# A four-layer graph network on one core: step table by products, norms folded into weights, work moved into the gather loops

## The chip, the core and the metric

The kernel runs on one core of a Trainium2 chip, as one program. The time is the device time of that core in microseconds. Before the change the runs took 7613.0, 7617.18 and 7625.78 us, median 7617.18.

## The reference

6250 nodes with 128 features and 106,250 edges, sorted by destination, pass through four layers, each added to its input and normalised: `x = layernorm(x + layer(x))`. The change concerns the first layer (two SAGE convolutions with batch norm) and what is prepared for it:

```
def _sage_conv(h, src, dst, n_nodes, Wl, bl, Wr):
    msg = jnp.take(h, src, axis=0)
    agg = jax.ops.segment_sum(msg, dst, num_segments=n_nodes)
    cnt = jax.ops.segment_sum(jnp.ones_like(src, dtype=h.dtype), dst, num_segments=n_nodes)
    agg = agg / jnp.clip(cnt, 1.0)[:, None]
    return agg @ Wl + bl + h @ Wr
def _batchnorm(h, gamma, beta):
    mu = jnp.mean(h, axis=0)
    var = jnp.mean((h - mu) ** 2, axis=0)
    return (h - mu) * jax.lax.rsqrt(var + EPS) * gamma + beta
...
h = _sage_conv(x, src, dst, n, Wl0, bl0, Wr0)      # 128 -> 256
h = _batchnorm(jax.nn.relu(h), g0, b0)
h = _sage_conv(h, src, dst, n, Wl1, bl1, Wr1)      # 256 -> 256
h = _batchnorm(jax.nn.relu(h), g1, b1)
return jax.nn.relu(h @ Wp + bp)                    # 256 -> 128
```

The other three (a Moebius aggregation, an equivariant convolution with weights from 64 edge features, graph attention) follow on the same edges and are untouched, except that edge weights for the last two are computed inside the SAGE loops.

## The kernel before

Nodes lie in 49 tiles of 128 (`TILES`, `NP` = 6272 columns), edges in 831 tiles of 128. A *step* is one pair of a node tile and an edge tile that meet; there are 880 (`STEPS`), in bodies of 8 (110 `BODIES`). The stages run one after the other, with a barrier between: `setup`, `sage_layer` for layers 0 and 1, `moebius`, `equivariant`, `gat`.

`setup` builds the pointer of each node into the edges: 49 VectorE passes compare the first destination of every edge tile (`firsts`, 832 columns) with the nodes of a tile, 49 GpSimd gathers fetch the edge tile in question (L336), and 49 more passes count in it. The pointers go through DRAM and back; from them come the degrees, the boundaries of node tiles, the step table (`stT`, node tile of a step; `stE`, edge tile), then gathers of `src` and `dst` for each step and transposes give `srcS` and `dstS`. A counting sort of the nodes by degree (`oh`, `cum`, `rank`) gives the place of each. Beside it x is split in three bf16 parts (L403 and on), each pass over all 6272 columns, and stored as `x_split`.

`sage_layer` has for each step an indirect DMA that GpSimd issues (L700): 128 rows of the split table, 16 slots deep (`SLOTS`). At every fourth step GpSimd waits until TensorE's `step_done` has freed slots. TensorE multiplies the three parts with a 128x128 one-hot matrix (L789: 3 matmuls in layer 0, 6 in layer 1). VectorE makes the one-hots for four steps at a time (L200) and adds each product into `agg` (L884). Between steps TensorE computes the edge weights for later layers (L798, L808, in layer 0 also L802), ScalarE moves them (L731). TensorE's, ScalarE's and VectorE's bodies are hardware loops (`fours`); GpSimd's 880 gathers are written out.

A tail follows. VectorE multiplies `agg` by 1/degree (L921). For 14 chunks (`NCH`) of 448 columns (`CH`) and two halves TensorE forms `agg` Wl + own Wr (L829, L831), ScalarE adds the bias and applies relu (L757), VectorE takes statistics (L937), then normalises both halves (L950). Layer 0 then transposes each tile (L841) and splits it in three parts (VectorE L957, L959; ScalarE L768, L770), stores `y_split`; meanwhile GpSimd scatters the sorted node table (L704). Layer 1 at its start loads that table (`sback`, copied at L867) and clears `span_src`; in its tail GpSimd reduces the largest degree (L709), VectorE plans the spans of `moebius`, GpSimd gathers 49 `span_src` (L1009), TensorE projects tile by tile (two products with Wp and one with the bias, L844, L845), VectorE applies relu and adds x (L962), and `LayerNorm` ends the stage. The order of work on each engine is the order of the code; engines meet at semaphores.

## Time and profile before

| | |
|---|---|
| median of three runs | 7617.18 us |
| the profiled execution | 7613.2 us |
| its span, first to last instruction | 7611.2 us |
| VectorE busy | 4112.7 us (54%) |
| GpSimd busy | 5148.9 us (68%) |
| TensorE busy | 2675.4 us (35%) |
| ScalarE busy | 1491.7 us (20%) |

In the rows below PE is TensorE, PEld its weight load, DVE VectorE, ACT ScalarE, POOL GpSimd and SP the engine that issues the remaining DMAs. L200 is line 200 of the kernel before; `out<-in` are the buffers by the program's names. A windows row gives a stretch in us from the span's start, its length, then for each engine its busy us and, in brackets, its instructions, then TensorE's granted clock as a share of full speed, the mean busy share of 16 DMA engines, and GB/s. A timeline row gives start, duration, engine, line, operation, names, the count, and in brackets how long the engine stood idle before it and what ended that. Issuing a DMA counts as "issue". A row of one line's instructions gives count, shortest/median/longest ns, first and last start. What is averaged over the span says little here: the stages have different limits, so the rows are taken stage by stage.

### The profile page before, as it was taken

How to read it: one execution, taken by the hardware profiler on the slowest of the kernel's cores; microseconds unless marked ns; L12 is line 12 of the kernel's file. 1: busy time of each engine (PE TensorE's matmuls, PEld its weight loads, DVE VectorE, ACT ScalarE, POOL GpSimd, SP SyncE). 2: the span in 40 equal slices, each digit the busy share in tenths (PEclk: the TensorE clock that was granted, in tenths of full speed). 3: DMA queues.
4: the chain of work that ended last, by engine and by line, in shares of the span. 5: the costliest groups of instructions: out<-in, count | busy, mean ns of one | idle time of the engine just before them, and what ended most of it. 6: DMA issues, size and time to landing. Idle time of an engine off the chain costs nothing. (4 is left out here: it accounts for less than half of the span.)

```text
span 7611.2 us, 86798 instructions
## 1 busy us (share of the span) xinstructions
PE 2675.4 (35%) x13121; PEld 1768.7 (23%) x13121; DVE 4112.7 (54%) x10643; ACT 1491.7 (20%) x5205; POOL 5148.9 (68%) x5017
## 2 busy tenths in 40 slices
PE   0466666756677673000000005666667100000000
PEld 0244444435455442000000003333335100000000
DVE  5344443454444433676677866777777414444465
ACT  0000000120000010121222104777774000000000
POOL 3277777757777742777777564777774477777765
PEclk9666555667777775555555557788878555555555
DMA  2544444356666621222222113333332322222211
GB/s 36 101 126 123 126 123 125 88 171 198 197 198 198 195 62 45 49 46 48 48 47 48 35 26 95 101 101 101 101 101 56 84 55 52 52 52 52 53 39 32
DMA packets 433517, 681.95 MB, mean 90 GB/s; under 512 B 159150, under 2 KB 266608, under 8 KB 433120
## 3 DMA queue, kind: packets, MB, share of 16 engines
q0 software_dynamic: 203280, 470.84, 24.5%
q10 hardware_dynamic: 127152, 159.46, 6.3%
q1 hardware_dynamic: 102944, 50.32, 2.9%
q14 instruction: 120, 0.98, 0.0%
q8 instruction: 21, 0.34, 0.0%
HBM read 584.78 MB, written 95.44 MB: 89 GB/s over the span
## 5 line engine op out<-in xcount | busy, mean ns | idle before, releaser
L1116 POOL DMA_INDIRECT mb_rows<-x_tab,mb_idx x906 | 1009.1, 1114 | 342.5 <-issue 276.4
L789 PE MATMUL ps<-onehot,rows 128*128 128x128 bf16 x7920 | 945.4, 272 | 732.7 <-DMA rows<-x_split,srcS 329.5
L884 DVE TENSOR_TENSOR agg<-agg,ps 128x128 f32 (+1 forms) x1760 | 623.7, 354 | 954.6 <-PE ps L789 806.3
L1414 POOL DMA_INDIRECT eq_frow<-f_tab,srcS x880 | 894.6, 1017 | 356.8 <-issue 267.9
L1732 POOL DMA_INDIRECT gt_rows<-h_tab,gt_idx x906 | 931.8, 1028 | 298.7 <-issue 273.9
L700 POOL DMA_INDIRECT rows<-x_split,srcS x880 | 864.8, 983 | 379.3 <-issue 244.9
L700 POOL DMA_INDIRECT rows<-y_split,srcS x880 | 840.6, 955 | 333.2 <-issue 245.8
L1436 ACT ACTIVATE eq_pb<-eq_wrow 128x64 f32<-128x64 f32 (+1 forms) x3520 | 864.1, 334 | 430.9 <-DVE eq_msg L1553 366.7
L1476 PE MATMUL eq_ps<-eq_msg,eq_onehot 128*128 128x320 f32 x1760 | 739.6, 581 | 435.2 <-DVE eq_onehot L200 423.8
L789 PEld LDWEIGHTS ps<-onehot,rows 128*128 128x128 bf16 x7920 | 631.6, 120 | 1106.2 <-DVE agg L884 738.9
L1464 PE MATMUL eq_ps<-ident,eq_x 128*128 128x128 f32 x49 | 14.0, 291 | 1686.9 <-DMA eq_m<-in_L_gnn_W_l_D 1686.9
L1476 PEld LDWEIGHTS eq_ps<-eq_msg,eq_onehot 128*128 128x128 f32 x1760 | 425.9, 254 | 748.4 <-DVE eq_acc L1561 570.7
L200 DVE TENSOR_TENSOR onehot<-iota,dstS 128x512 bf16<-128x512 f32 x440 | 305.3, 694 | 275.3 <-issue 263.0
L1561 DVE TENSOR_TENSOR eq_acc<-eq_acc,eq_ps 128x320 f32 x880 | 425.0, 483 | 51.6 <-issue 29.8
L808 PE MATMUL ps<-w2d,hT 128*128 128x256 f32 x880 | 415.8, 624 | 0.0
L1464 PEld LDWEIGHTS eq_ps<-ident,eq_x 128*128 128x128 f32 x49 | 7.3, 151 | 1688.7 <-issue 1687.2
L731 ACT ACTIVATE wrow<-ps 128x512 f32<-128x512 f32 x220 | 131.3, 597 | 1268.7 <-PE ps L808 1268.7
L1845 DVE TENSOR_TENSOR gt_alpha<-gt_rows,gt_scores_in 128x196 f32<-128x196 f32 (+5 forms) x36 | 9.5, 264 | 671.5 <-DMA gt_rows<-h_tab,gt_idx 671.0
L1179 DVE TENSOR_TENSOR mb_prod<-mb_rows,mb_xd 128x256 f32<-128x256 f32 (+4 forms) x128 | 140.5, 1098 | 401.8 <-DMA mb_rows<-x_tab,mb_idx 322.3
L1153 ACT ACTIVATE mb_rows<-mb_rows,mb_gm 128x128 f32<-128x128 f32 x906 | 268.5, 386 | 361.6 <-DVE mb_gm L1222 361.6
L1009 POOL DMA_INDIRECT span_src<-in_src,span_at x147 | 161.0, 1095 | 243.3 <-DVEq L1805 158.5
L1548 DVE TENSOR_TENSOR eq_msg<-eq_pb,eq_frow 128x512 f32<-128x512 f32 x220 | 152.4, 693 | 259.5 <-DMA eq_frow<-f_tab,srcS 248.2
(395 smaller groups left out, 5021.9 us busy)
## 6 DMA issues: line engine op xcount, KB each, us to landing
eq_wrow<-w_tab ACTq DMA_DIRECT2D x223, 264.0 KB, 3.0
w_tab<-wrow ACTq DMA_DIRECT2D x220, 264.0 KB, 2.7
es<-in_side ACTq DMA_DIRECT2D x220, 136.0 KB, 2.6
mb_rows<-x_tab,mb_idx POOLq DMA_INDIRECT x906, 2.6
gt_rows<-h_tab,gt_idx POOLq DMA_INDIRECT x906, 2.5
rows<-x_split,srcS POOLq DMA_INDIRECT x880, 2.7
rows<-y_split,srcS POOLq DMA_INDIRECT x880, 3.1
eq_frow<-f_tab,srcS POOLq DMA_INDIRECT x880, 2.6
```

What stands on the lines that cost most here:

```text
L200: return dve.tensor_tensor(onehot[:, 4 * half:4 * half + 4], broadcast(s["iota"][:], four, 1), broadcast(s["dstS"][:, bass.ds(4 * b, 4)], ...
L700: pool.indirect_dma_start(rows[:, n % SLOTS, :], None, table, bass.IndirectOffsetOnAxis(ap=s["srcS"][:, n:n + 1], axis=0)).then_inc(gather ...
L789: last = pe.matmul(ps[:, u % 4, f * P:(f + 1) * P], rows[:, slot, at:at + P], onehot[:, u], start=(part == 0), stop=(part == 2))
L808: last = pe.matmul(ps[:, 7, 2 * n * P:(2 * n + 2) * P], hT[:, n * P:(n + 1) * P], w2d[:], start=True, stop=True)
L884: dve.tensor_tensor(into, into, ps[:, u % 4, 0:W].rearrange("p (k n) -> p k n", n=P), ALU.add).then_inc(added, 1)
L1116: pool.indirect_dma_start(rows[:, r, n, :], None, t["x1"], bass.IndirectOffsetOnAxis(ap=idx[:, r, n:n + 1], axis=0)).then_inc(gathered[r][ ...
L1153: act.activation(rows[:, r, n, 0:D], rows[:, r, n, 0:D], ACT.Copy, scale=gm[:, n:n + 1]).then_inc(scaled_ready, 1 if n + 1 < UPTO[p] else ...
L1414: pool.indirect_dma_start(frow[:, n % SLOTS, :], None, t["f"], bass.IndirectOffsetOnAxis(ap=s["srcS"][:, n:n + 1], axis=0)).then_inc(gathe ...
L1436: last = act.activation(pb[:, r % 2, u, f].rearrange("p c w -> p (c w)"), wrow[:, r, bass.ds(at, 1), lo:lo + 64].rearrange("p o f -> p (o ...
L1476: pe.matmul(ps[:, 4 * r + u, 0:MC], onehot[:, 4 * r + u], msg[:, r, u], start=True, stop=True).then_inc(step_done, 1)
L1561: dve.tensor_tensor(into, into, ps[:, 4 * (r % 2) + u, 0:MC], ALU.add).then_inc(added, 1)
L1732: pool.indirect_dma_start(rows[:, r, n, :], None, t["h"], bass.IndirectOffsetOnAxis(ap=idx[:, r, n:n + 1], axis=0)).then_inc(gathered[r][g ...
```

## The change

**Setup.** The inputs get an array `first`, the first destination of each edge tile, copied to all partitions. One counting pass over 896 columns gives for each of 49 tiles how many edge tiles start below it; from it comes `reach`, a 0/1 matrix of tile by step, whose column sum (a product with ones) less 1 is `stT`; `stE` is the step's number less `stT`. `srcS` and `dstS` are products of the edge arrays with one-hot matrices (`pick`) of `stE`, in four quarters. The split of x is cut in 7 groups and shared by ScalarE and VectorE. Pointers, degrees and the sort leave setup.

**First layer** (`sage_first`). One more matmul with one column for each step counts edges, in column P of `agg`. In bodies 4 to 52 TensorE also forms x Wr + bias of a tile (`h0`). The tail goes by tile: product with `wl`, VectorE multiplies by 1/degree and adds `h0`, ScalarE and VectorE split relu of it; `y_split` holds the unnormalised values, and `h0` is stored too.

**Second layer** (`sage_second`). In the loop `h0` is loaded and transposed (bodies 2 to 26), its statistics taken, and the norm folded into `wl`, `wr`, `cvec` and `bwl`; the own part (three 448-column products for each of 28 half chunks) follows at even bodies from 34. Histogram and placement of the sort are spread over bodies 2 to 14 and from 35 on. The scatters of the sorted table, its reload, the span plan stand behind this layer's loop. The dense tail takes the mean in 14 pieces, two products for each half chunk, and folds the second norm into `wps` and a bias that VectorE adds. Loops of TensorE and ScalarE (both layers) and of VectorE (second layer) are written out. The core of the diff (the old code stands above):

```diff
-            "ptr": dram("ptr_tab", (NP + P,), I32),
             "rc": dram("rc_tab", (NP,)),
-            "stepT": dram("step_node_tile", (EROWS,), I32),
-            "stepE": dram("step_edge_tile", (EROWS,), I32),
+            "h0": dram("h0_tab", (NP, HID)),
...
+            pe.wait_ge(reach_ready, 1)
+            for h in range(2):
+                last = pe.matmul(ps[:, h, 0:2 * QUART], s["ones_h"][0:TILES, :], reach[0:TILES, h * 2 * QUART:(h + 1) * 2 * QUART],
+                                 start=True, stop=True)
+            last.then_inc(counted, 1)
+            for q in range(4):
+                pe.wait_ge(pick_ready, q + 1)
+                for n in range(2):
+                    for j, c in enumerate(chunks[q]):
+                        last = pe.matmul(ps[:, 2 + q, 256 * n:256 * n + QUART], edge_f[:, n, c], pick[q][:, j], start=(j == 0),
+                                         stop=(j == len(chunks[q]) - 1))
+                last.then_inc(picked, 1)
...
+            dve.wait_ge(first_in, 16)
+            do(dve.tensor_scalar(junk[0:TILES], first_i[0:TILES], part128[0:TILES], 0.0, ALU.is_lt, ALU.add,
+                                 accum_out=cnt[0:TILES]))
+            do(dve.tensor_scalar(bound[0:TILES], cnt[0:TILES], -1.0, 0.0, ALU.add, ALU.max))
+            do(dve.tensor_tensor(bound[0:TILES], bound[0:TILES], part_f[0:TILES], ALU.add))
+            do(dve.tensor_scalar(reach[0:TILES], col_f[0:TILES], bound[0:TILES], None, ALU.is_ge))
+            dve.sem_inc(reach_ready, 1)
+            dve.wait_ge(edges_in, 32)
+            for n in range(2):
+                do.put(dve.tensor_copy(edge_f[:, n], edge_i[:, n]))
+            dve.wait_ge(counted, 1)
+            for h in range(2):
+                do.put(dve.tensor_scalar(stT[:, h * 2 * QUART:(h + 1) * 2 * QUART], ps[:, h, 0:2 * QUART], -1.0, None, ALU.add))
+            do.sync()
+            do(dve.tensor_tensor(stE[:], col_f[:], stT[:], ALU.subtract))
+            for q in range(4):
+                for j, c in enumerate(chunks[q]):
+                    do.put(dve.tensor_scalar(pick[q][:, j], stE[:, q * QUART:(q + 1) * QUART], row_f[:, c:c + 1], None, ALU.is_equal))
+                do.sync()
+                dve.sem_inc(pick_ready, 1)
...
+            for g in range(GROUPS + 1):
+                if g < GROUPS:
+                    dve.wait_ge(hi_ready, g + 1)
+                    dve.tensor_tensor(rest[:, seven(g)], xin[:, seven(g)], xs[:, seven(g), 0], ALU.subtract).then_inc(rest_ready, 1)
+                if g < 4:
+                    steps(g)
+                if g:
+                    dve.wait_ge(mid_ready, g)
+                    dve.tensor_tensor(xs[:, seven(g - 1), 2], rest[:, seven(g - 1)], xs[:, seven(g - 1), 1],
+                                      ALU.subtract).then_inc(xs_ready, 1)
...
+                    pe.matmul(ps[:, u % 4, P:P + 1], onehot[:, u], s["ones_h"][:, 0:1], start=True, stop=True)
+                    for part in range(3):
+                        last = pe.matmul(ps[:, u % 4, 0:P], rows[:, slot, part * D:(part + 1) * D], onehot[:, u],
+                                         start=(part == 0), stop=(part == 2))
                     last.then_inc(step_done, 1)
...
                 last.then_inc(w_psum, 1)
...
+                if PRE <= k < PRE + TILES:
+                    if k == PRE:
+                        pe.wait_ge(setup_in, N_SETUP)
+                    n = k - PRE
+                    pe.matmul(ps[:, 5, HID:2 * HID], xT[:, n * P:(n + 1) * P], wr[:], start=True, stop=False)
+                    pe.matmul(ps[:, 5, HID:2 * HID], s["ones"][0:1, :], bl[:], start=False, stop=True).then_inc(pre_psum, 1)
+                steps(k, 4, 6)
...
+            pe.wait_ge(added, STEPS + 4)
             for n in range(TILES):
...
+                if n >= 4:
+                    pe.wait_ge(summed, n - 3)
+                pe.matmul(ps[:, n % 4, 0:HID], agg[:, n, 0:P], wl[:], start=True, stop=True).then_inc(dense_ready, 1)
...
+            dve.wait_ge(pre_ready, TILES)
+            for n in range(TILES + 2):
+                if n < TILES:
+                    dve.wait_ge(dense_ready, n + 1)
+                    dve.scalar_tensor_tensor(h0[:, n], ps[:, n % 4, 0:HID], rc[:, n:n + 1], h0[:, n], ALU.mult,
+                                             ALU.add).then_inc(summed, 1)
+                if 1 <= n <= TILES:
+                    dve.wait_ge(hi_ready, n)
+                    if n > 3:
+                        dve.wait_ge(staged, n - 3)
+                    dve.scalar_tensor_tensor(yrest[:, (n - 1) % 3], h0[:, n - 1], 0.0, ystage[:, (n - 1) % G, 0], ALU.max,
+                                             ALU.subtract).then_inc(rest_ready, 1)
+                if n >= 2:
+                    dve.wait_ge(mid_ready, n - 1)
+                    dve.tensor_tensor(ystage[:, (n - 2) % G, 2], yrest[:, (n - 2) % 3], ystage[:, (n - 2) % G, 1],
+                                      ALU.subtract).then_inc(staged, 1)
...
+        TURN = 2
+        HIST = TURN + QUADS4 + 2
+        CONST = TURN + PAIRS + 4
+        OWN = CONST + 3
+        PLACE = OWN + 1
+        PLACED = PLACE + 2 * QUADS4 + 1
...
+            pool.wait_ge(rank_ready, 1)
+            for n in range(TILES):
+                pool.indirect_dma_start(t["srt"][:, :], bass.IndirectOffsetOnAxis(ap=s["rank"][:, n:n + 1], axis=0),
+                                        s["sval"][:, n, :], None).then_inc(sorted_out, 16)
+            pool.wait_ge(deg_ready, 1)
+            pool.partition_all_reduce(dmax[:], s["sdeg"][:], P, bass.bass_isa.ReduceOp.max).then_inc(dmax_ready, 1)
+            pool.wait_ge(plan_ready, 1)
+            for n in range(TILES):
+                span_sources(pool, a, s, n).then_inc(span_in, 16)
...
+            def turn_pair(j):
+                pe.wait_ge(yT_ready, j)
+                for m in range(2):
+                    n = 2 * j + m
+                    if n < TILES:
+                        pe.wait_ge(hin_in[n % 4], 16 * (n // 4) + 16)
+                        for f in range(2):
+                            last = pe.transpose(ps[:, 6, 256 * f + P * m:256 * f + P * m + P], hin[:, n % 4, half(f)], s["ident"][:])
+                last.then_inc(turned, 1)
+
+            def own_part(j):
+                c, f = j // 2, j % 2
+                pe.wait_ge(pre_ready, j)
+                if f == 0:
+                    pe.wait_ge(sign_ready, c + 1)
+                for k in range(2):
+                    pe.matmul(ps[:, 6, 0:CH], wr[:, k, half(f)], yT[:, k, chunk(c)], start=(k == 0), stop=False)
+                pe.matmul(ps[:, 6, 0:CH], bwl[:, half(f)], sign[:, c % 2], start=False, stop=True).then_inc(pre_psum, 1)
...
+                if k >= OWN and (k - OWN) % 2 == 0 and (k - OWN) // 2 < 2 * NCH:
+                    if k == OWN:
+                        pe.wait_ge(w_scaled, 1)
+                    own_part((k - OWN) // 2)
+                if k >= PLACE and (k - PLACE) % 2 == 0 and (k - PLACE) // 2 < QUADS4:
+                    b = (k - PLACE) // 2
+                    pe.wait_ge(place_in, b + 1)
+                    many = min(4, TILES - 4 * b)
+                    for m in range(many):
+                        place = ps[:, 4, m * P:(m + 1) * P]
+                        pe.matmul(place, s["ones_h"][:], cum[:, m], start=True, stop=False)
+                        last = pe.matmul(place, s["tri"][:], oh[:, m], start=False, stop=True)
+                    last.then_inc(place_ready, 1)
+                steps(k, 4, 8)
...
+            pe.wait_ge(pre_ready, 2 * NCH + 1)
+            for n in range(2 * NCH):
+                c, f = n // 2, n % 2
+                if f == 0:
+                    pe.wait_ge(mean_ready, c + 1)
+                if n >= 4:
+                    pe.wait_ge(sum_ready, n - 3)
+                for k in range(2):
+                    last = pe.matmul(ps[:, n % 4, 0:CH], wl[:, k, half(f)], agg[:, k, chunk(c)], start=(k == 0), stop=(k == 1))
...
+                if 0 <= k - TURN < QUADS4:
+                    for m in range(key_hot(k - TURN)):
+                        do(dve.tensor_tensor(cum[:, 0], cum[:, 0], oh[:, m], ALU.add))
...
+            for k in range(BODIES):
+                h, i = k % BUFS, k // BUFS
                 for u in range(U):
+                    b = 2 * k + u // 4
                     if u % 4 == 0:
...
+                        tiles = node_tiles(dve, s, b)
+                        if 2 <= b + 1 < 2 * BODIES:
+                            one_hots(b + 1)
+                    add(U * k + u, tiles[u % 4])
                     if u == 1:
...
                         dve.wait_ge(es_in[h], 16 * i + 16)
...
+                        if i:
                             dve.wait_ge(w_out[h], 16 * i)
...
+                        dve.tensor_copy(wrow[:, h, :, D:WW],
+                                        es[:, h, 2 * P:SIDE].rearrange("p (n f) -> p n f", n=WB)).then_inc(e4_ready, 1)
+                    if u == 3:
+                        side(k)
...
+            mean(0)
+            mean(1)
+            dve.wait_ge(pre_ready, 2 * NCH + 1)
             for c in range(NCH):
+                if c + 2 < NCH:
+                    mean(c + 2)
                 for f in range(2):
-                    dve.wait_ge(dense_free, 2 * c + f + 1)
-                    do.put(dve.bn_stats(stats[:, f, c], h_[:, f, c * CH:min((c + 1) * CH, N)]))
+                    n = 2 * c + f
+                    dve.wait_ge(dense_ready, n + 1)
+                    dve.tensor_tensor(yT[:, f, chunk(c)], ps[:, n % 4, 0:CH], yT[:, f, chunk(c)], ALU.add).then_inc(sum_ready, 1)
+                    if c:
+                        tally(n - 2)
...
+            def order():
+                dve.wait_ge(sorted_in, 16)
+                do.put(dve.tensor_copy(s["perm"][:], sback[:, :, 0]))
+                do.put(dve.tensor_copy(s["eptr"][:], sback[:, :, 1]))
+                do(dve.tensor_copy(s["sdeg"][:], sback[:, :, 2]))
+                dve.sem_inc(deg_ready, 1)
...
+            order()
             for n in range(TILES):
...
+                dve.wait_ge(projected, n + 1)
+                dve.wait_ge(x_in[n % G], 16 * (n // G + 1))
+                do(dve.tensor_tensor(v[:, n], ps[:, n % G, 0:D], bias, ALU.add))
+                dve.scalar_tensor_tensor(v[:, n], v[:, n], 0.0, xin[:, n % G], ALU.max, ALU.add).then_inc(staged, 1)
+                if n == G:
+                    plan()
```

GpSimd, from the first layer's gathers to the end of the second layer; before:

```order
L693 UNCONDITIONAL_BRANCH
L700 DMA rows<-x_split,srcS 128x384 x880
L704 DMA sorted_nodes<-sval,rank_i 6272x4 x49
L540 UNCONDITIONAL_BRANCH
L76 ISA
L693 UNCONDITIONAL_BRANCH
L700 DMA rows<-y_split,srcS 128x768 x880
L709 ISA
L709 ISA dmax<-sdeg 128x49
L1009 DMA span_src<-in_src,span_at 128x48 x49
```

and after the change (names of the layers' buffers now begin with `s_`):

```order
L521 UNCONDITIONAL_BRANCH
L526 DMA s_rows<-x_split,srcS 128x384 x880
L433 UNCONDITIONAL_BRANCH
L76 ISA
L838 UNCONDITIONAL_BRANCH
L843 DMA s_rows<-y_split,srcS 128x768 x880
L847 DMA sorted_nodes<-sval,rank_i 6272x4 x49
L850 ISA
L850 ISA s_dmax<-sdeg 128x49
L1241 DMA span_src<-in_src,span_at 128x48 x49
```

The 49 scatters moved from behind the first layer's gathers to behind the second's, ahead of the reduction (`dmax`) and the span gathers.

VectorE, around a one-hot in the second layer's body; before:

```order
L884 TENSOR_TENSOR agg<-agg,ps 128x2x128
L193 TENSOR_LOAD stepT
L193 ISA x2
L200 TENSOR_TENSOR onehot<-iota,dstS 128x512
L884 REGISTER_ALU
L884 ISA
L884 TENSOR_TENSOR agg<-agg,ps 128x2x128
```

and after, in one of bodies 2 to 14:

```order
L1023 TENSOR_TENSOR s_agg<-s_agg,s_ps 128x2x128
L1028 TENSOR_TENSOR s_oh<-iota,s_key 128x512
L1049 TENSOR_TENSOR s_cum<-s_cum,s_oh 128x128 x4
L194 TENSOR_LOAD stepT
L194 ISA x2
L201 TENSOR_TENSOR s_onehot<-iota,dstS 128x512
L1023 REGISTER_ALU
L1023 ISA
L1023 TENSOR_TENSOR s_agg<-s_agg,s_ps 128x2x128
```

A one-hot of sort keys and four additions now stand between the fourth addition of a body and the next one-hot.

TensorE, a body of the second layer; before:

```order
L798 MATMUL ps<-es,w1d 128x256
L784 ISA
L785 ISA
L789 MATMUL ps<-onehot,rows 128x128 x6
L785 REGISTER_ALU
L789 MATMUL ps<-onehot,rows 128x128 x6
L785 REGISTER_ALU
L789 MATMUL ps<-onehot,rows 128x128 x6
L785 REGISTER_ALU
L789 MATMUL ps<-onehot,rows 128x128 x6
L805 REGISTER_ALU
L808 MATMUL ps<-w2d,hT 128x256 x2
```

and after, in a body that also holds an own part:

```order
L943 MATMUL s_ps<-s_es,s_w1d 128x256
L916 MATMUL s_ps<-s_onehot,s_rows 128x128 x24
L948 MATMUL s_ps<-s_w2d,s_hT 128x256 x2
L936 MATMUL s_ps<-s_yT,s_wr 128x448 x2
L937 MATMUL s_ps<-span_src,s_bwl 128x448
L916 MATMUL s_ps<-s_onehot,s_rows 128x128 x24
```

The own part's three products stand behind the side products, between a body's first four steps and its last four (24 matmuls each); register work of the loop is gone.

## Rows read from the trace of the kernel before

**Rows 1.** Windows by stage: length, busy PE, PEld, DVE, ACT, POOL; clock, DMA, GB/s

```profile
0.00:326.70 326.70, 56.49 (x218) 34.94 (x218) 147.70 (x331) 0.68 (x2) 74.63 (x75) 0.88 0.30 39
326.70:1463.20 1136.50, 733.44 (x3734) 499.47 (x3734) 461.45 (x1432) 108.44 (x221) 864.81 (x880) 0.59 0.45 130
1463.20:1594.90 131.70, 75.89 (x216) 37.09 (x216) 71.98 (x142) 53.13 (x129) 58.62 (x49) 0.68 0.23 79
1594.90:2710.50 1115.60, 755.99 (x5922) 559.23 (x5922) 542.46 (x1214) 108.42 (x221) 840.66 (x881) 0.77 0.67 197
2710.50:2981.50 271.00, 180.18 (x536) 114.36 (x536) 103.94 (x384) 19.16 (x37) 46.70 (x51) 0.67 0.11 30
2981.50:7611.20 4629.70, 873.46 (x2495) 523.59 (x2495) 2785.19 (x7142) 1201.83 (x4597) 3263.45 (x3084) 0.59 0.25 61
```

**Rows 2.** GpSimd's timeline at the borders of the stages

```profile
326.70 0.94 POOL L700 DMA_INDIRECT rows<-x_split,srcS  x1 [107.90 <-POOLq L77]
...
350.28 0.94 POOL L700 DMA_INDIRECT rows<-x_split,srcS  x1 [3.92 <-PE ps L789]
...
1594.91 0.98 POOL L700 DMA_INDIRECT rows<-y_split,srcS  x1 [58.45 <-POOLq L77]
...
1621.94 0.94 POOL L700 DMA_INDIRECT rows<-y_split,srcS  x1 [7.28 <-PE ps L789]
...
2710.45 0.47 POOL L709 PARTITION_ALL_REDUCE dmax<-sdeg  x1 [0.21 <-issue]
...
2981.49 0.94 POOL L1104 DMA_INDIRECT mb_xd<-x_tab,perm  x1 [186.74 <-PEq L1043]
```

**Rows 3.** The gathers of the first loop, by source line

```profile
L700 POOL DMA_INDIRECT rows<-x_split,srcS x880: 940/946/1462, 326.7 to 1462.0; - x176
```

**Rows 4.** Timelines of VectorE and GpSimd, setup and second loop

```profile
80.64 6.69 DVE L404 TENSOR_TENSOR rest<-xin,xs 128x6272 f32<-128x6272 f32 x1
80.75 7.41 POOL L336 DMA_INDIRECT drow<-in_dst,blk_i  x1 [0.30 <-issue]
...
2002.56 0.69 DVE L200 TENSOR_TENSOR onehot<-iota,dstS 128x512 bf16<-128x512 f32 x1 [0.51 <-issue]
2002.62 1.44 POOL L700 DMA_INDIRECT rows<-y_split,srcS  x1 [0.30 <-issue]
```

**Rows 5.** VectorE's timeline at the start of setup

```profile
9.29 0.17 DVE L374 MEMSET ones<- 128x128 f32 x1 [9.15 <-POOL last_i L331]
...
18.34 1.08 DVE L396 TENSOR_SCALAR_CACHE_REDUCE junk<-firsts,node_f 128x832 f32<-128x832 f32 x1 [3.33 <-POOL firsts L333]
```

**Rows 6.** Windows in the second tail: dense products, then the projection

```profile
2728.00:2817.00 89.00, 86.84 (x224) 43.55 (x224) 20.66 (x61) 16.73 (x29) 46.27 (x49) 0.97 0.09 14
2828.00:2919.00 91.00, 90.37 (x290) 68.54 (x289) 14.45 (x50) 0.00 (x0) 0.00 (x0) 0.50 0.11 31
```

**Rows 7.** DMA issues of the page: count, us from issue to landing

```profile
rows<-x_split,srcS POOLq DMA_INDIRECT x880, 2.7
```

**Rows 8.** VectorE's timeline in the first tail

```profile
1467.25 6.69 DVE L921 TENSOR_TENSOR agg<-agg,rcb 128x6272 f32<-128x6272 f32 x1
...
1530.92 0.43 DVE L959 TENSOR_TENSOR ystage<-yrest,ystage 128x256 bf16<-128x256 f32 x1 [0.47 <-ACT ystage L770]
1531.26 0.42 DVE L957 TENSOR_TENSOR yrest<-ps,ystage 128x256 f32<-128x256 f32 x1
...
1590.28 0.42 DVE L959 TENSOR_TENSOR ystage<-yrest,ystage 128x256 bf16<-128x256 f32 x1 [0.47 <-ACT ystage L770]
```

**Rows 9.** VectorE's timeline: second tail, and the table's load

```profile
2714.94 13.29 DVE L921 TENSOR_TENSOR agg<-agg,rcb 128x6272 f32<-128x6272 f32 x2
...
2918.41 0.29 DVE L962 SCALAR_TENSOR_TENSOR yT<-ps,xin 128x128 f32<-128x128 f32 x1 [1.58 <-PE ps L845]
...
1601.09 0.20 DVE L867 COPY perm<-sback 128x49 int32<-128x49 int32 x1 [6.33 <-DMA sback<-sorted_nodes]
```

**Rows 10.** The scatters of the sorted table, by source line

```profile
L704 POOL DMA_INDIRECT sorted_nodes<-sval,rank_i x49: 965/969/6632, 1463.2 to 1535.5; - x49
```

1153 lines of the change are left out of this document (600 added, 553 removed).

## The prediction, made before the changed kernel was run

> **What bounds the kernel now.** I first cut the span at the stages' borders with the windows view [rows 1], taking the borders from GpSimd's timeline [rows 2]. The reader is to see six stretches: setup up to the first gather (326.7 us), the first layer's loop (1136.5), its tail (131.7), the second layer's loop (1115.6), its tail (271.0), and the rest (4629.7), which the change doesn't touch. The change can only win or lose in the first five, 2981.5 us together.
>
> In both loops the bound is GpSimd. Each of 880 gathers has a median of 946 ns [rows 3] and is followed by 0.30 us of issue, the gap that the timeline shows before most of them [rows 2]. That makes 1.249 us, and 880 of them 1099 us. The loops take 1136.5 and 1115.6, so 37.5 and 16.6 us lie above that floor. Of these 3.6 and 7.0 us are one wait each near the start, where the 17th gather waited for TensorE's first steps (3.92 and 7.28 us less the usual 0.30) [rows 2]. The rest, 34 and 10 us, are gathers that took longer. [Rows 4] show why: a VectorE tensor_tensor of 6.69 us that reads two SBUF operands began at 80.64, and the indirect DMA begun at 80.75 lasted 7.41 us, to the end of that pass. In the loop the 0.69 us one-hot of 2002.56 stretched the gather of 2002.62 to 1.44 us. The additions into `agg`, which read PSUM and SBUF, leave no such trace. TensorE is busy 733 of 1136 and 756 of 1116 us, VectorE 461 and 542 [rows 1], and their order only matters where it makes GpSimd wait.
>
> In setup and in the tails GpSimd is not the bound: a chain of VectorE, TensorE and round trips through DRAM is.
>
> **Setup.** All of the old chain goes: 49 counting passes of 1.08 us over 832 columns [rows 5] plus 49 over the fetched blocks, 49 gathers of blocks, the pointer table's way to DRAM and back, the step table's, and the node sort. The new chain: VectorE starts as before at 9.3 us, when GpSimd's iotas are there [rows 5]. One counting pass over 896 columns costs 1.2 us by the same row. I estimate about 2 us for bounds and `reach`, 1.3 for two casts, 1.5 for `stT`, 1 for `stE`, 3.5 for 11 compares of 224 columns, and 4 for the small tables: 24 us. Then x is split in 7 groups. A pass over 6272 columns takes 6.69 us [rows 4], so 0.96 per group, two of them on VectorE and two now on ScalarE beside it; four groups also carry two copies of 224 columns (0.7 us). That is 4 x 2.6 + 3 x 1.9 + 1 = 17 us, to 41. The products on TensorE (22 of 224 columns, about 0.4 us each at the high clock, 0.8 at the low, half of the 448-column ones in [rows 6]) need 9 to 17 us from about 18 on and lie beside it. The last group's store, the barrier and the first issue take some 8 us: first gather at 50, against 326.7. Bounds: 40 if the small operations are cheaper, 72 if ScalarE or TensorE gates the groups. **-277**, between -255 and -287.
>
> **The two start waits.** In the new first layer the one-hots precede the wait for the attention weights, and the loads of side data are issued first; 16 gathers take 20 us and TensorE's first steps should be done by then. In the second layer the wait for the sorted table and the clearing of `span_src` are gone from VectorE's head, leaving its 10.5 us clearing of `agg`. Both waits vanish, **-10**; if they stay, 0.
>
> **What moves into the loops.** First layer: one matmul with one column for each step, and 49 bodies with two 256-column products. Second layer: 98 transposes, 28 own parts of three 448-column products, 98 small placement products, and on VectorE two sets of 13 key one-hots and 98 cumulative additions. TensorE: the old second tail ran 224 instructions in 86.84 us [rows 6], two for each 448-column product, so 0.78 each: 84 x 0.78 = 65 us, with the small ones about 120 us at the high clock, 240 at the low; idle are 360 us [rows 1]. First layer: about 90 for the products and 90 for the counts, idle 403. Both fit on the average. The largest lump, side product and own part at the low clock, is 2 + 4.7 us; GpSimd gathers up to 12 steps (15 us) ahead of TensorE, less 3 for the landing (2.7 [rows 7]), so the lump is covered. The order rows show these lumps stand between step 3 and step 4 of a body. ScalarE is busy 108 us of either loop and can take copies.
>
> What isn't covered is the shared port. Now 220 one-hots per loop cost 34 us in the first (0.155 each) and 10 in the second (0.045): the phase against the gather decides. The count matmul makes a step's result some 0.1 us later, towards the gather's start, where a one-hot hurts more; lumps of TensorE scatter the phase. I take +8 in the first loop. The second gets 26 key one-hots, 98 short additions and 13 masks with two SBUF operands, plus a less lucky phase: +14. Together **+22**. Bounds: -43 if no one-hot ever meets a gather; +155 if each of 440 costs 0.45 us as the one in [rows 4] did.
>
> The Trainium skill speaks against moving such work here: "SBUF — State Buffer", section "SBUF: two separate sides", says that a VectorE operation with two SBUF inputs and a GpSimd operation take their shared port pair exclusively, each for its whole length, and the loser stands still. The trace agrees [rows 4]. By the rule alone all added two-operand time (18 + 26 + 9 us) could come on top, some +53; what it costs here hangs on whether the gather begins inside it.
>
> **First tail.** Before: mean, 56 products, statistics, normalisation, transposes, split. The statistics, normalisation and transposes go. For each tile VectorE now has three passes of 256 columns. Such passes started 0.34 us apart where none waited (1530.92 to 1531.26 [rows 8]), but the pair took 1.24 us with ScalarE's hop; the new loop is skewed over three tiles so that the hop lies beside other work: 3 x 0.35 = 1.05 us, 49 + 2 rounds 54 us. The stores grow from 192 to 320 KB a tile, 16.1 MB in all. The second loop moves 197 GB/s at a DMA share of 0.67 [rows 1], so 294 at full share and 55 us. Both limits meet; I take 56. Before it stand 4.1 us of last steps (1463.2 to 1467.25 [rows 8]) and an estimated 2.1 of small passes for the reciprocals, behind it 7.5 for a last store of 7 tiles and the barrier (4.2 before, from 1590.7 to 1594.9 [rows 2, 8]). 69.7 instead of 131.7: **-62**. With stores at 197 GB/s it would be 82 + 14, so -36; without any waiting -66.
>
> **Second tail.** Here two things move against each other. VectorE and TensorE: the mean pass (13.3 us [rows 9]) is cut into 14 pieces beside TensorE, half of the dense products are gone (1.55 us a half chunk instead of 3.1), normalisation (7 us) and the bias product too. VectorE then bounds with 0.96 for the mean and 0.56 for each of two additions and two statistics of 448 columns (13.29 us for 2 x 6272 columns make 1.06 ns each, and an estimated 0.08 to start), 3.2 us a chunk: 4.5 + 2 + 45 + 9 for the rest up to the projection = about 60 us after the last gather. But the 49 scatters of the sorted table, in the old first tail hidden beside dense work, now stand behind the last gather on GpSimd's queue [rows 2], and VectorE's wait for the table stands ahead of every projection tile. They took 58.6 us of work [rows 1] and 49 x 0.30 of issue, 73.3 together, of which 11 were two of them held beside long passes (median 0.969, the longest 6.632 [rows 10], beside the 6.69 us pass of 1467.25 [rows 8]); at the median it is 62, and I take 67. Landing 2.5, loading the table back 6.8 (VectorE waited 6.33 of it [rows 9]), unpacking 0.7: 77. So the table, not the products, releases the projection, 17 us late. The projection ran 49 tiles in 91 us with 6 instructions each at the 1.2 GHz level (clock 0.50) [rows 6]; now 4: 1.24 us a tile. Seven tiles are ready, 42 x 1.24 + 1 = 53: 130. VectorE's plan of 5 us lies inside TensorE's seven-tile lead, and the 49 `span_src` gathers (61 us) end at about 149. From the last tile to the next stage 62.8 us are as before (2918.7 to 2981.5 [rows 2, 9]): 193 instead of 271, **-78**. If the clock were high there, VectorE's 0.65 us a tile would bound and it would be -103; if the scatters took 78, -65.
>
> **Sum.** -277 - 10 + 22 - 62 - 78 = -405 us. The profiled execution took 7613.2 us (span 7611.2), so 7208; the median of the runs is 7617.2, 4 us above, so I predict 7210.
>
> **Rivals.** (a) The shared port bites: the new step time puts the one-hots just ahead of each gather, 0.45 instead of 0.1 us, in both loops. For it: the one-hot of [rows 4] and the port rule; against: each delay moves the gather itself, and neither loop of before sat there. 7208 + 133 = about 7340. (b) TensorE's lumps are not covered: if each of the 28 own parts and 49 pre-products costs its low-clock length in full (28 x 4.7 + 49 x 1.9), that is +220, half of it likely: 7320. Against: the 12-step lead. (c) Everything lucky: no contention, high clock in the projection: 7210 - 65 - 25 = 7120. (d) Slower than before. TensorE's, ScalarE's and the second layer's VectorE bodies, looped before, are now written out 110 times. If each body cost a stall of fetching code on TensorE beyond its idle time, so that a body of 8 steps takes more than 10.1 + 1.9 us, the 220 bodies would eat all 405. At 12.5 us it is +528: 7740. Against it: GpSimd's 880 gathers were written out too, and their gap stays at 0.30 [rows 2]; TensorE has 3 us idle per body.
> The Trainium skill, "Runtime: NRT & Kernel Launch", section "Instruction fetch mechanics", says that fetching is sequential and prefetched and that taken branches break it, so by it the written-out code costs nothing, against (d). The even gaps of the gathers agree; no row shows TensorE that way.
>
> **Chances.** Forecast 0.74 (7150 to 7270), (a) 0.09, (b) 0.08, (c) 0.06, (d) 0.03. The range for 8 in 10 reaches towards (a), (b) and (c): 7140 to 7310. Faster by over 0.2% (15 us, about what a measurement of this kernel can tell from none): 0.96; within 0.01; slower 0.03.
>
> **What would show it.** First gather at about 50 us; the 17th gather of each loop without a wait; loops of 1141 and 1123 us with GpSimd's gap at 0.30 and the excess in gather durations beside one-hots and key one-hots; the second loop's first gather 70 us after the first's end; in the second tail 49 scatters with VectorE waiting for `sback` until some 76 us, then a tile each 1.24 us at clock 0.50; everything behind that as before within 5 us. I am wrong if GpSimd waits for TensorE in the loops by more than a few us, if setup ends after 75 us, or if the second tail is above 215.

## The result, and the profile after

The changed kernel took 7212.69 us (median of four, 7207.55 to 7217.6) against 7616.94 for the kernel before on the same chip: ratio 0.9468, 95% interval 0.9451 to 0.9484. The forecast was 7210. The profiled execution took 7207.55 us, its span is 7205.6, and its windows, cut at the same borders as [rows 1], read (length, busy PE, PEld, DVE, ACT, POOL, clock, DMA share, GB/s):

```profile
0.00:49.60 49.60, 11.59 (x46) 10.05 (x46) 30.13 (x66) 14.62 (x17) 1.56 (x9) 0.85 0.65 190
49.60:1181.20 1131.60, 774.83 (x4807) 546.10 (x4807) 458.18 (x1430) 126.46 (x270) 863.28 (x880) 0.65 0.46 128
1181.20:1260.30 79.10, 36.85 (x110) 17.82 (x108) 55.25 (x159) 35.98 (x99) 0.00 (x0) 0.80 0.89 212
1260.30:2403.50 1143.20, 787.28 (x6307) 583.13 (x6308) 623.49 (x1474) 145.06 (x290) 875.10 (x881) 0.80 0.67 201
2403.50:2574.80 171.30, 77.87 (x332) 53.52 (x328) 126.44 (x479) 21.72 (x38) 100.84 (x99) 0.71 0.22 48
2574.80:7205.60 4630.80, 874.25 (x2495) 526.73 (x2495) 2780.40 (x7142) 1201.83 (x4597) 3258.69 (x3084) 0.59 0.25 61
```

| stage | before | forecast | measured | off by |
|---|---|---|---|---|
| setup | 326.7 | 50 | 49.6 | -0.4 |
| first loop | 1136.5 | 1141 | 1131.6 | -9 |
| first tail | 131.7 | 69.7 | 79.1 | +9 |
| second loop | 1115.6 | 1123 | 1143.2 | +20 |
| second tail | 271.0 | 193 | 171.3 | -22 |
| rest | 4629.7 | 4629.7 | 4630.8 | +1 |

So the total is right to 3 us, while four of the five changed stages are off by 9 to 22 us and cancel. These four are what the experiments are about.

GpSimd's timeline shows the first surprise, one row in each loop. Both waits of the 17th gather, 3.92 and 7.28 us in [rows 2], are gone; instead the first gather of each loop lasts 8.04 and 14.32 us, where it took 0.94 and 0.98:

```profile
49.62 8.04 POOL L526 DMA_INDIRECT s_rows<-x_split,srcS  x1 [37.25 <-POOLq L77]
...
1260.31 14.32 POOL L843 DMA_INDIRECT s_rows<-y_split,srcS  x1 [79.51 <-POOLq L77]
```

VectorE at the same time, with two one-hots directly behind the clearing of `agg`:

```profile
1262.77 10.51 DVE L1009 MEMSET s_agg<- 128x12544 f32 x1 [2.56 <-issue]
1273.19 1.22 DVE L201 TENSOR_TENSOR s_onehot<-iota,dstS 128x512 bf16<-128x512 f32 x2
```

In the kernel before the same clearing stood from 1607.5 to 1618.0, gathers were issued beside it, and none took more than 0.95 us; there a semaphore wait stood between it and the one-hots. The row's start has to be read with care: VectorE cleared 256 columns just before in 0.27 us, and at that rate 12544 take about 13.1 us (an estimate), which is the 10.51 us of the row and the 2.56 us in front of it. So the clearing began, by that estimate, at about 1260.2, just ahead of the gather.

The second is in the first tail. The rounds of three VectorE passes follow at 1.06 us each, as forecast, up to the eighth tile, and there VectorE stands still; the second row is from the view of ScalarE's waits in that stretch (us in total, times, longest):

```profile
1208.69 0.42 DVE L703 SCALAR_TENSOR_TENSOR s_yrest<-s_h,s_ystage 128x256 f32<-128x256 f32 x1 [13.94 <-ACT s_ystage L564]
```

```profile
ACT s_ystage L564 <- DMA y_split<-s_ystage: 15.6, 2, 14.8
```

ScalarE waits for the first tile's store. From 1186 to 1208 us the DMA view has this line,

```profile
DMA packets 7011, 1.00 MB, mean 46 GB/s; under 512 B 6379, under 2 KB 7010, under 8 KB 7010
```

and of SyncE's issues in it these two:

```profile
y_split<-s_ystage SPq DMA_DIRECT2D x6, 192.0 KB, 10.8
rc_tab<-s_rc SPq DMA_DIRECT2D x1, 24.5 KB, 21.6
```

`rc_tab` are the reciprocal degrees, 24.5 KB in elements of 4 bytes: 6272 of the packets. SyncE now stores them ahead of the first tile, and they took 21.6 us to land.

The third is the projection. VectorE gets the table 75 us behind the last gather, as forecast (76), after 13.75 us of waiting; but then the tiles do not take 1.24 us each:

```profile
2478.32 0.20 DVE L1176 COPY perm<-s_sback 128x49 int32<-128x49 int32 x1 [13.75 <-DMA s_sback<-sorted_nodes]
```

The windows over the projection, same columns as above:

```profile
2488.60:2494.00 5.40, 4.79 (x22) 4.79 (x23) 4.92 (x20) 0.00 (x0) 4.11 (x5) 0.50 0.40 100
2494.00:2500.00 6.00, 6.00 (x50) 6.00 (x49) 5.62 (x24) 0.00 (x0) 4.62 (x5) 0.89 0.55 134
2500.00:2507.00 7.00, 7.00 (x63) 6.99 (x63) 6.55 (x28) 0.00 (x0) 5.33 (x6) 1.00 0.61 152
```

After the pause the clock is at the 1.2 GHz level (0.50) and rises to 2.4 GHz within the projection; in [rows 6] it stood at 0.50 for all of 91 us. At the high level a tile takes 0.53 us, and VectorE's two passes are what sets it.

For the loops I compared each gather with its median of 946 ns and added up what lies above it, the held first gathers apart. It is 24.4 us in the first loop (before 32.9) and 30.0 in the second (before 9.0). Sorted by the VectorE operation that ran when the gather began, 25 of the second loop's 30 us stand beside one-hots: 84 gathers that a one-hot lengthened by more than 0.05 us, 25.2 us in all, 0.30 each. With 1099 us of floor and the 7.1 and 13.4 us of the held gathers that makes 1130.5 and 1142.4, within 1 us or so of the loops (1131.6 and 1143.2).

### The profile page after: what moved, and what is told of

Same layout as the page of the kernel before. It is cut to its first block and busy times, and to the rows that moved or that the text cites. A ratio compares the mean times of both kernels' runs of the same rounds, so it can differ in the third digit from the quotient of the medians.

```text
span 7205.6 us, 84694 instructions
## 1 busy us (share of the span) xinstructions
PE 2562.7 (36%) x14090; PEld 1737.3 (24%) x14090; DVE 4073.9 (57%) x10750; ACT 1545.7 (21%) x5308; POOL 5099.5 (71%) x4952
## 5 line engine op out<-in xcount | busy, mean ns | idle before, releaser
L843 POOL DMA_INDIRECT s_rows<-y_split,srcS x880 | 875.1, 994 | 347.3 <-issue 251.0
L526 POOL DMA_INDIRECT s_rows<-x_split,srcS x880 | 863.3, 981 | 305.2 <-issue 251.4
L1023 DVE TENSOR_TENSOR s_agg<-s_agg,s_ps 128x256 f32 x880 | 369.7, 420 | 446.9 <-PE s_ps L916 314.8
L916 PE MATMUL s_ps<-s_onehot,s_rows 128*128 128x128 bf16 x5280 | 488.7, 251 | 324.7 <-DMA s_rows<-y_split,srcS 302.1
L659 DVE TENSOR_TENSOR s_agg<-s_agg,s_ps 128x129 f32 x880 | 254.6, 289 | 524.4 <-PE s_ps L585 432.6
L916 PEld LDWEIGHTS s_ps<-s_onehot,s_rows 128*128 128x128 bf16 x5280 | 385.0, 114 | 467.4 <-DMA s_rows<-y_split,srcS 408.0
L201 DVE TENSOR_TENSOR s_onehot<-iota,dstS 128x512 bf16<-128x512 f32 x440 | 304.7, 693 | 217.7 <-issue 171.2
L585 PE MATMUL s_ps<-s_onehot,s_rows 128*128 128x128 bf16 x2640 | 359.5, 272 | 0.0
```

Of the source, the lines that this page charges most:

```text
L201: return dve.tensor_tensor(onehot[:, 4 * half:4 * half + 4], broadcast(s["iota"][:], four, 1), broadcast(s["dstS"][:, bass.ds(4 * b, 4)], ...
L526: pool.indirect_dma_start(rows[:, n % SLOTS, :], None, t["xs"], bass.IndirectOffsetOnAxis(ap=s["srcS"][:, n:n + 1], axis=0)).then_inc(gath ...
L585: last = pe.matmul(ps[:, u % 4, 0:P], rows[:, slot, part * D:(part + 1) * D], onehot[:, u], start=(part == 0), stop=(part == 2))
L843: pool.indirect_dma_start(rows[:, n % SLOTS, :], None, t["ys"], bass.IndirectOffsetOnAxis(ap=s["srcS"][:, n:n + 1], axis=0)).then_inc(gath ...
L916: last = pe.matmul(ps[:, u % 4, half(f)], rows[:, slot, at:at + P], onehot[:, u], start=(part == 0), stop=(part == 2))
L1023: dve.tensor_tensor(into, into, ps[:, n % 4, 0:HID].rearrange("p (k n) -> p k n", n=P), ALU.add).then_inc(added, 1)
```

## The experiments

Where an experiment's effect is small, its stages are compared by the profile, from the start of one gather to another, since medians from different chips scatter by some 10 us. "Less than the changed kernel" below is the difference of its gain over the kernel before on its own chip to the 404 us of the changed kernel.

**A wait between the clearing and the one-hots** (`e1_wait_zero`).

```diff
             dve.sem_inc(added, 4)
+            dve.wait_ge(agg_zero, 1)
             def compare(b):
...
+            dve.wait_ge(agg_zero, 1)
             one_hots(0)
             one_hots(1)
-            dve.wait_ge(agg_zero, 1)
```

> The changed kernel with VectorE's wait for the end of the clearing of agg moved ahead of the first two one-hots, in both SAGE layers; nothing else. In the changed kernel the first gather of each loop took 8.04 and 14.32 us instead of 0.94. Theory Q (queued lock): a one-hot with two SBUF operands that stands ready right behind the clearing holds the port from then on, and the gather waits for both; then with the wait between them both first gathers take under 1.7 us, the loops are 1124 and 1130 us (now 1131.6 and 1143.2) and the time falls by about 20 us. Theory M (the clearing itself holds the gather): both stay at 8 and 14 us, no change. Theory F (the first gather behind a barrier is slow in itself in this code): no change either.

Measured: 7188.03 us, ratio 0.9444 (0.9427 to 0.9460), 17 us less than the changed kernel. GpSimd and VectorE at the second loop's start:

```profile
1255.40 0.95 POOL L843 DMA_INDIRECT s_rows<-y_split,srcS  x1 [79.65 <-POOLq L77]
```

```profile
1257.86 10.51 DVE L1009 MEMSET s_agg<- 128x12544 f32 x1 [2.56 <-issue]
1268.40 1.29 DVE L201 TENSOR_TENSOR s_onehot<-iota,dstS 128x512 bf16<-128x512 f32 x2
```

Clearing and one-hots are as long as ever; only the wait stands between, and the gather takes 0.95 us (1.30 in the first loop), as do the ones behind it that run beside the clearing. From first to last gather's start the loops went from 1130.2 to 1124.6 and from 1141.9 to 1130.2 us. Neither the clearing itself nor the first gather in itself is the cause: what makes the difference is whether an operation stands ready behind the clearing. How such an operation can hold a gather before it has started itself, the runs don't show. In the second loop the excess of the other gathers stayed, at 31.6 us.

**The reciprocal degrees as rows** (`e2_rc_rows`).

```diff
-            sp.dma_start(t["rc"].rearrange("(t p o) -> p t o", p=P, o=1), rc[:].unsqueeze(2),
-                         allow_slow_non_contiguous=True).then_inc(rc_out, 16)
...
+                if n == 6:
+                    sp.wait_ge(rc_ready, 2)
+                    sp.dma_start(t["rc"].rearrange("(t p) -> t p", p=P), rcT[0:TILES, :]).then_inc(rc_out, 16)
...
+                    pe.transpose(ps[0:TILES, 6, 2 * P:3 * P], rc[:], s["ident"][:]).then_inc(rc_turned, 1)
```

> The changed kernel with the reciprocal degrees transposed on TensorE and stored as 49 rows of 512 bytes behind the seventh tile's store, instead of 6272 elements of 4 bytes ahead of the first. The first tail is 79.1 us in the changed kernel, with one stall of 13.9 us at the eighth tile, where ScalarE waits for the first tile's store. Theory R: the stall is the small elements ahead of it in SyncE's queue; then it goes, the tail is 66 to 70 us, and the time falls by 9 to 13. Theory B (the bytes: 16.1 MB at the rate of the engines): the stall only spreads over the later tiles, the tail stays above 76 us and the time within 3 us.

Measured: 7190.07 us, ratio 0.9447 (0.9431 to 0.9463), 15 us less. The same wait of ScalarE, and the packets of the same 22 us:

```profile
ACT s_ystage L566 <- DMA y_split<-s_ystage: 1.4, 2, 0.8
```

```profile
DMA packets 4252, 5.12 MB, mean 233 GB/s; under 512 B 295, under 2 KB 4251, under 8 KB 4251
```

From the last gather of the first loop to the first of the second it is 66.9 us instead of 80.4. The 16 MB alone are hidden: theory R holds. The edit changes two things, though, the form of the store and its place behind the seventh tile, and no run takes them apart; that the form matters is read from the 21.6 us that these 24.5 KB took in the changed kernel.

**The table's wait moved into the projection** (`e3_table_late`).

```diff
+                if n == TABLE - 4:
+                    sp.wait_ge(sorted_out, 16 * TILES)
+                    sp.dma_start(sback[:], t["srt"].rearrange("(t p) f -> p t f", p=P)).then_inc(sorted_in, 16)
...
             for n in range(TILES):
+                if n == TABLE:
+                    order()
```

> The changed kernel with the wait for the sorted table (order) at projection tile 28 instead of ahead of the first, and SyncE's load of it moved to the same place in its row. In the changed kernel VectorE waits 13.75 us for the table while TensorE has 7 tiles ready. Theory T (the table is what releases the projection): the wait shrinks below 2 us, the last projection tile ends 10 to 13 us earlier, and since the span gathers (61 us from the plan on) keep their place and end ahead of the LayerNorm, the second tail falls from 171 to about 160. Rival C (clock): the pause is what left TensorE at its high level in the projection; without it the tiles take 1.24 us at the low level as before the change (49 tiles, 61 us), and the tail gets longer, about 185.

Measured: 7202.94 us, ratio 0.9463 (0.9447 to 0.9479): no difference that the runs can tell. By the profile the tail, from last gather to the next stage's first, fell from 172.6 to 167.1, where about 160 was expected. TensorE's timeline and a window:

```profile
2467.69 17.62 PE L1003 MATMUL s_ps<-s_wps,s_yT 128*128 128x128 f32 x124
2489.64 8.23 PE L1003 MATMUL s_ps<-s_wps,s_yT 128*128 128x128 f32 x48 [4.32 <-DVE s_agg L1196]
```

```profile
2465.00:2482.00 17.00, 15.86 (x107) 14.53 (x107) 13.15 (x44) 0.00 (x0) 11.53 (x12) 0.82 0.33 62
```

The 13.75 us wait is gone, but 4.3 us of it came back: VectorE waited 4.42 us for a load of x, and SyncE's loads stand behind its wait for the scatters. Half of the gain was there, not all. Rival C is out: without the pause the clock is 0.82.

**One-hots of the second loop as four tensor_scalar** (`e4_scalar_hots`).

```diff
+    for u in range(4):
+        last = dve.tensor_scalar(onehot[:, 4 * half + u], s["iota"][:], s["dstS"][:, 4 * b + u:4 * b + u + 1], None, ALU.is_equal)
+    last.then_inc(ready, 1)
...
-                one_hot(dve, s, onehot, b, b % 2).then_inc(onehot_ready, 1)
+                four_hots(dve, s, onehot, b, b % 2, onehot_ready)
```

> The changed kernel with each one-hot of the second SAGE layer (one tensor_tensor of 512 columns with two SBUF operands) made by four tensor_scalar of 128 columns, which read one tensor and a number for each partition. Port theory: only operations with two SBUF operands hold a gather; the one-hots account for some 25 of the 30.8 us by which the second loop's gathers exceed 946 ns, the key one-hots and placement for the other 5, and the first gather's 14.3 us go too, since no one-hot with two operands stands behind the clearing: second loop 1143 to about 1105, the time down by 35 to 40 us. Rival L (any long VectorE operation beside a gather's start holds it): the excess stays at 25 or grows with the longer passes (4 x 0.28 instead of 0.69), no gain or a few us slower.

Measured: 7175.38 us, ratio 0.9430 (0.9415 to 0.9446), 30 us less. The excess beside one-hots fell from 25.2 to 1.7 us (24 gathers by more than 0.05 us), that of the whole loop from 30.0 to 7.4. But the first gather was held as before, by operations with only one tensor operand:

```profile
L850 POOL DMA_INDIRECT s_rows<-y_split,srcS x880: 942/946/13858, 1262.8 to 2382.6; - x176
```

```profile
1275.65 1.53 DVE L201 TENSOR_SCALAR s_onehot<-iota,dstS 128x128 bf16<-128x128 f32 x8
```

So the port theory is right on the loop's excess and wrong on the first gather: one-hots with one tensor operand behind the clearing hold it too. It ended at 1276.63, before the last of the eight one-hots (1277.18), so not all of them were waited for. Whether the small excess is owed to the kind of the operations or to their length, the next one asks.

**The same with four short tensor_tensor** (`e10_short_pairs`).

```diff
-        last = dve.tensor_scalar(onehot[:, 4 * half + u], s["iota"][:], s["dstS"][:, 4 * b + u:4 * b + u + 1], None, ALU.is_equal)
+        last = dve.tensor_tensor(onehot[:, 4 * half + u], s["iota"][:], s["dstS"][:, 4 * b + u:4 * b + u + 1].broadcast_to([P, P]),
+                                 ALU.is_equal)
```

> The changed kernel with each one-hot of the second loop made by four tensor_tensor of 128 columns, both operands in SBUF, instead of one of 512; beside the kernel that made them by four tensor_scalar, where the gathers stretched beside a one-hot fell from 25 to 2 us. Theory K (the kind of the operation: only two tensors from SBUF hold a gather): the four stand one behind the other for 0.85 us, and the excess of the gathers beside them stays at 20 us or more; second loop 1140 to 1145. Theory L (the length: a gather is held to the end of the operation that runs, and gets in between two short ones): the excess falls to 6 us or less as with tensor_scalar, second loop about 1120 with the first gather's 14 us still in it.

This one and `e9_one_row` ran on a chip where the kernel before took 8740.59 us, and the engines have issue gaps that no other run shows; their times say little, 8347.31 us and a ratio of 0.9556 (0.9497 to 0.9615), and the loop's length can't be compared. The gathers' durations can: their median is 949 ns, and beside one-hots the excess is 4.5 us in 42 gathers, 0.11 each. In the first loop of the same run, where the one-hots still had 512 columns, 69 gathers lost 0.28 each, and in the changed kernel's second loop 84 lost 0.30. VectorE and GpSimd at one such meeting:

```profile
2005.65 0.90 DVE L201 TENSOR_TENSOR s_onehot<-iota,dstS 128x128 bf16<-128x128 f32 x4 [0.24 <-PE s_ps L924]
```

```profile
2005.72 1.05 POOL L851 DMA_INDIRECT s_rows<-y_split,srcS  x1 [0.31 <-issue]
```

0.90 us of two-operand work, and the gather that began 0.07 us into it lost 0.10. Theory L holds in the main: the length of one operation decides, not the sum of those that follow each other. The kind may have a smaller share. Over all gathers that began beside a one-hot, lengthened or not, the mean loss is 0.22 us with one of 512 columns (117 gathers), 0.05 with four tensor_tensor of 128 (111) and 0.02 with four tensor_scalar (149), the middle one from the other chip.

**Own parts three times over** (`e5_own_thrice`).

```diff
+                for again in range(3):
+                    for k in range(2):
+                        pe.matmul(ps[:, 6, 0:CH], wr[:, k, half(f)], yT[:, k, chunk(c)], start=(k == 0), stop=False)
+                    last = pe.matmul(ps[:, 6, 0:CH], bwl[:, half(f)], sign[:, c % 2], start=False, stop=True)
```

> The changed kernel with each own part in the second loop (three products of 448 columns) issued three times over, so a lump of 9 instead of 3 at 28 places, 168 more products of about 0.78 us at the high clock. Theory of the forecast (12 gathered steps cover a lump): a lump grows from 2.3 to 7 us at the high clock and 14 at the low; GpSimd's waits for TensorE grow by less than 10 us and the loop stays within 1143 to 1155. Rival (b) of the prediction (lumps are not covered, each costs its length): 28 x 4.7 = 130 us more in the second loop, about 1270.

Measured: 7235.86 us, ratio 0.9524 (0.9509 to 0.9538), 43 us more than the changed kernel. From first to last gather the second loop took 1174.3 us, 32 more. GpSimd's wait for TensorE in it (total, times, longest; 16.7 us in 55 times in the changed kernel, which is the usual 0.3 each):

```profile
POOL s_rows L843 <- PE s_ps L916: 61.1, 84, 3.2
```

The rival's 130 us are out, and so are my 10: the cover ends between a lump of 3 products, which cost nothing, and one of 9. The other 11 of the 43 us lie outside this loop, and no stage accounts for them; they are of the size of the scatter between chips.

**x in one piece** (`e6_x_whole`).

```diff
-            for g in range(GROUPS):
-                sp.dma_start(xin[:, seven(g)], by_group(a["x"])[g]).then_inc(x_in[g], 16)
+            sp.dma_start(xin[:], a["x"].rearrange("(t p) d -> p t d", p=P)).then_inc(x_in[0], 16)
...
+            do(dve.tensor_copy(xs[:, :, 0], xin[:]))
+            do(dve.tensor_tensor(rest[:], xin[:], xs[:, :, 0], ALU.subtract))
+            do(dve.tensor_copy(xs[:, :, 1], rest[:]))
+            do(dve.tensor_tensor(xs[:, :, 2], rest[:], xs[:, :, 1], ALU.subtract))
```

> The changed kernel with x loaded, split and stored in one piece on VectorE alone, ahead of the step table's last copies, as in the kernel before, instead of in 7 groups shared with ScalarE. The step table by products stays. Theory: of the 277 us that setup lost nearly all is the table's chain, and the groups are worth 25 to 30 us: four passes of 6.69 us one after the other from about 24 us on, to 51, then one store of 4.8 MB in some 20 us and the barrier, first gather at about 78 instead of 49.6. Rival: splitting x in groups is what counts, since its store then overlaps; the first gather would come at 100 or later.

Measured: 7225.39 us, ratio 0.9510 (0.9495 to 0.9524), 33 us more; by the profile 20.6 of them are in setup, the rest is not found in any one stage. VectorE's passes, and the gathers that follow:

```profile
25.29 6.67 DVE L341 CAST xs<-xin 128x6272 bf16<-128x6272 f32 x1
...
45.44 6.69 DVE L344 TENSOR_TENSOR xs<-rest,xs 128x6272 bf16<-128x6272 f32 x1
```

```profile
L516 POOL DMA_INDIRECT s_rows<-x_split,srcS x880: 942/946/8037, 70.2 to 1200.6; - x176
```

Apart from the last copies (2.5 us from 52.3 on) the table's work on VectorE is over at 25.3 us, and the first gather comes at 70.2. So the groups are worth 21 us once the old chain is gone, less than the 25 to 30 expected, and some 256 of the 277 us belong to the table's chain with the sort.

**Dense products twice** (`e8_dense_twice`).

```diff
+                for again in range(2):
+                    for k in range(2):
+                        last = pe.matmul(ps[:, n % 4, 0:CH], wl[:, k, half(f)], agg[:, k, chunk(c)], start=(k == 0), stop=(k == 1))
```

> The changed kernel with each of the 56 dense products of the second tail issued twice (the second overwrites the first with the same sum), nothing else. My prediction took the projection at the 1.2 GHz level, 1.24 us a tile, as 224 instructions in 87 us at a granted clock of 0.97 had stood before it; in the changed kernel 112 stand there and the projection ran at 0.82, VectorE-bound, 0.53 us a tile. Theory W (the work ahead sets the level): with 224 instructions, some 88 us, ahead of it the projection runs at 0.50 again, 1.2 us a tile: the tail is 171 + 37 for the products + 28 for the projection - 14 for the table's wait, which is now covered, about 222. Rival S (fewer instructions in each tile, with TensorE waiting for VectorE between, keep it high): the tiles stay at 0.53 us, tail about 195.

Measured: 7231.21 us, ratio 0.9518 (0.9503 to 0.9533), 38 us more. The tail took 201.4 us from last gather to next stage, 172.6 in the changed kernel: 29 of the 38. Windows in the projection:

```profile
2503.00:2513.00 10.00, 10.00 (x60) 9.78 (x61) 7.84 (x26) 0.00 (x0) 0.53 (x1) 0.68 0.16 45
2518.00:2527.00 9.00, 8.88 (x58) 8.88 (x59) 8.30 (x34) 0.00 (x0) 6.87 (x8) 0.71 0.50 123
2527.00:2537.00 10.00, 9.92 (x81) 9.43 (x79) 9.22 (x38) 0.00 (x0) 7.56 (x9) 1.00 0.55 140
```

224 instructions in 86.24 us stood ahead, as in [rows 6], and the clock still rose: theory W is out.

**The one-row product put back** (`e9_one_row`).

```diff
+                pe.matmul(ps[:, n % G, 0:D], s["ones"][0:1, :], none[:], start=False, stop=True).then_inc(projected, 1)
```

> The changed kernel with a third product in each projection tile, one row of ones by a row of zeros, where the kernel before had its bias product; the sums are the same. Twice the dense work ahead of the projection did not bring back the 1.2 GHz level (granted clock 0.68 to 1.00 there), and the wait for the table is not what keeps it high either (0.82 without it). What is left of the difference to the kernel before, which stood at 0.50 for all of 91 us though TensorE was 97 to 100% busy, is this product. Theory O: with it a third of the time goes to products of one row, and the clock stays at 0.50: 1.86 us a tile as before, the projection's 42 later tiles take 78 instead of some 23 us, the second tail about 226 instead of 171. Rival N: the product only adds its own time, some 0.3 us a tile at the high level, the clock rises to 0.8 or more as in the changed kernel, tail about 180.

Measured: 8380.8 us, ratio 0.9591 (0.9544 to 0.9639), on the slow chip named above, so the tail's length proves nothing. Windows of the projection in which TensorE was busy all the time:

```profile
2901.00:2915.00 14.00, 14.00 (x46) 10.64 (x46) 6.93 (x19) 0.00 (x0) 0.52 (x1) 0.50 0.10 29
2915.00:2930.00 15.00, 15.00 (x50) 11.41 (x49) 8.76 (x49) 0.00 (x0) 5.90 (x6) 0.50 0.20 44
```

The granted clock stays at 0.50, with 46 instructions in 14 us: 1.83 us a tile, as before the change. It stayed there to the projection's end at 3032. On the same chip the `e10_short_pairs` kernel, without that product, had 0.74 over the projection's first 29 us, though TensorE was idle a third of them; from 2940 on it stood still most of the time, at 0.50. A window of those 29 us:

```profile
2925.00:2940.00 15.00, 10.46 (x64) 9.68 (x64) 8.64 (x35) 0.00 (x0) 10.98 (x12) 0.73 0.37 88
```

Theory O holds, for what stands in these tiles. Whether it is the product's one row that keeps the clock low, or that it is a third product in the tile, was not tried (a third one of 128 rows would tell), and why the runs don't say.

**All four repairs** (`e7_all_four`): the wait of the first experiment, the rows of the second, four tensor_scalar in both loops, and the table read by ScalarE's queue, with the wait for it at tile 20.

```diff
+            act.wait_ge(sorted_out, 16 * TILES)
+            act.dma_start(sback[:], t["srt"].rearrange("(t p) f -> p t f", p=P)).then_inc(sorted_in, 16)
...
+        TABLE = 20
...
+                if n == TABLE:
+                    order()
```

> The changed kernel with four edits together: VectorE's wait between the clearing of agg and the first one-hots (20 us by its own run), the reciprocal degrees stored as 49 rows (14 us by the profile of its own run), the one-hots of both loops as four tensor_scalar of 128 columns (in the second loop 23 us of the gathers' excess by its own run; the first loop has 25 us of excess, of which I expect 20 back), and the sorted table read by ScalarE's queue, with VectorE's wait for it at projection tile 20 (10 us, since SyncE's row of x loads is no longer held). If the stalls are separate, 20 + 14 + 23 + 20 + 10 = 87 us less than the changed kernel's 7212.7, so about 7126. If the one-hots' longer stay on VectorE in the first loop (4 x 0.28 us beside 8 additions, the erow and eh passes, in a hardware loop) makes TensorE late, the first loop keeps its 1125 us or grows, and the time is 7145 or more.

Measured: 7112.61 us, ratio 0.9363 (0.9350 to 0.9376), 80 us less than the changed kernel. Its windows by stage:

```profile
0.00:49.30 49.30, 11.17 (x46) 9.70 (x46) 30.12 (x66) 14.62 (x17) 1.57 (x9) 0.84 0.66 191
49.30:1153.10 1103.80, 797.97 (x4808) 557.26 (x4808) 495.45 (x2090) 126.40 (x270) 835.56 (x880) 0.62 0.47 132
1153.10:1218.40 65.30, 35.90 (x109) 17.94 (x108) 55.34 (x160) 36.39 (x99) 0.04 (x1) 0.86 0.75 257
1218.40:2326.60 1108.20, 772.42 (x6303) 573.65 (x6304) 665.09 (x2134) 144.73 (x290) 840.01 (x881) 0.82 0.70 208
2326.60:2488.40 161.80, 77.45 (x335) 52.47 (x332) 126.73 (x479) 21.89 (x38) 100.98 (x100) 0.72 0.25 51
2488.40:7106.40 4618.00, 867.51 (x2495) 520.56 (x2495) 2781.11 (x7142) 1201.85 (x4597) 3251.80 (x3084) 0.59 0.25 61
```

The loops are at 1103.8 and 1108.2 us, 5 and 9 us above the floor of 1099; the stages named in the expectation gave 28, 14, 35 and 9.5 us, 86 together against 87 expected. The other 13 us of the profile lie in the untouched rest, 4618.0 here and between 4617 and 4631 in the changed kernel and the other experiments on like chips; I count them as scatter.

## Why the prediction was right, and where it was not

**Setup** held to 0.4 us, and by the chain that was forecast: VectorE's last split pass ended at 42.8 us (forecast 41), the first gather came 6.8 us later (forecast 8).

**The two start waits.** That they vanish was right, that this is worth 10 us was not: the order of code that removed them (one-hots ahead of the wait, directly behind the clearing) holds the first gathers for 7.1 and 13.4 us, 20.5 together. I had looked at what VectorE no longer waits for, not at what now stands ready behind a long pass. With the wait put back in front of the one-hots the held gathers are gone and the 17th gather still does not wait.

**Contention in the loops.** I took +8 and +14, +22 together, for the gathers' excess; measured are 24.4 - 32.9 = -8.5 in the first loop and 30.0 - 9.0 = +21 in the second, +12.5 together. The bounds and the mechanism were right (the excess stands beside one-hots), the step "+8 in the first loop" had the sign wrong, and that the sum lies near is luck of phase. In the first loop one-hots lengthened fewer gathers by more than 0.05 us (119, before 184), in the second many more (84, before 26). Most of the second's growth is the one-hots that were there before, not the added key one-hots and placement passes, which cost about 4 us. The Trainium skill, "SBUF — State Buffer", section "SBUF: two separate sides", names two kinds of passes that hold GpSimd, each for its whole length: those with two SBUF inputs and those in a two-port performance mode. That the length decides agrees (0.30 us for a gather lengthened by a pass of 512 columns, 0.11 by passes of 128). The gather of 13.86 us behind a clearing and tensor_scalar passes with one tensor operand is no case of two inputs; in which mode those passes ran, no run here shows.

**TensorE's lumps** (rival b) cost nothing: GpSimd's wait for TensorE is 16.7 us in 55 times, none above its 0.3 of issue. Tripled, they cost 32 us, so the cover of 12 steps is real but not far from its end. Written-out bodies (rival d) cost nothing here either: the gap between gathers is still 0.30.

**First tail.** The step that failed is "both limits meet; I take 56". VectorE's rounds were right (1.06 us) and the bytes are hidden behind them; what I left out is a transfer that the change moves: the reciprocal degrees, in setup before, stand ahead of the tiles in SyncE's row, 6272 packets. They cost 13.9 us, 13.5 of which came back when they were stored as rows behind the seventh tile. The forecast terms themselves were 4.5 us too long together: 69.7 + 13.9 is 83.6, and 79.1 was measured. My count of what is stored went by megabytes, and these are 25 KB.

**Second tail.** The table's arrival was right to 1 us. The step that failed is "42 x 1.24": I carried over the clock of the old projection. I had worked out the other case, VectorE-bound tiles and -103 instead of -78, and gave it to a side branch; measured is -99.7. From the table to the last tile it took 32.5 us (2478.3 to 2510.8), where 53 was forecast. What kept the old projection at 1.2 GHz was not the work ahead of it, nor the pause, but the bias product of one row that stood in each of its tiles, as a third one, and that the change takes out.

The sum came out because +20 and +9 stood against -22 and -9.

## What to carry over

Look at what stands ready directly behind a long VectorE pass: with nothing between them GpSimd's DMA issue can be held to the end of that pass and beyond, and a semaphore wait in between cost nothing here. Where one-hots and gathers shared a loop, four short ones took more of VectorE's time and less in all. Count a moved transfer in packets, not in bytes, and follow the queue that it enters.

## What the runs showed of the hardware

- A clearing of 10.5 us with a one-hot queued behind it held a gather for 13.4 us more than its 0.95; with a semaphore wait between them 0, though gathers ran beside the clearing. One tensor operand behind it did nearly the same as two (13.86 and 14.32 us).
- Gathers lengthened beside a 512-column one-hot lost 0.30 us on the mean, beside 128-column ones 0.07 to 0.11.
- 24.5 KB as 6272 packets of 4 bytes took 21.6 us to land and the wait for the tiles' stores behind it was 14 us; 1.00 MB moved in 22 us. Stored as 49 rows of 512 bytes behind the seventh tile, they let 5.12 MB through.
- With only two products of 128 rows in its tiles the projection ended at a granted clock of 1.00, in the changed kernel and in the one with the dense work doubled; with a one-row product as the third in every tile it stayed at 0.50 throughout, in the kernel before (TensorE busy 90.4 of 91 us) and in the one that put the product back (busy for all of the first 29 us).
